# A two-layer GNN on one core: the tail after the edge loop in another order, and buffers of its own for the last edge pair

## The chip, the cores and the metric

The kernel runs on one core of a Trainium2 chip. The time is device microseconds of one execution. Of the kernel before there are three timed runs (median 1211.6 us) and one profiled execution of its own. PE is TensorE, DVE VectorE, ACT ScalarE, POOL GpSimd, SP SyncE.

## What is computed

There are 1250 nodes (padded to 1280, so 10 node tiles of 128) with 512 features, and 20000 edges. The first layer (a GIN block with batch norms) ends long before the change. The second layer is what matters here:

```python
h = jnp.maximum(_layernorm(x, axis=-1), 0.0)
edge_feat = jnp.concatenate([h[src], h[dst], edge_attr], axis=-1)
m = mish(mish(edge_feat @ W1 + b1) @ W2 + b2)       # 20000 x 512 messages
agg = jax.ops.segment_sum(m, dst, num_segments=h.shape[0])
u = mish(jnp.concatenate([h, agg], axis=-1) @ W3 + b3)
y = h + u @ W4 + b4
x = x + layernorm(y) * gamma + beta
```

## The kernel before

Every engine has one program, written out by hand in the order in which it runs; engines wait for each other by semaphores alone. Each f32 product is three fp32r products (high x low, low x high, high x high), so every operand is split first: a cast makes the high part, a subtraction the low part.

**The edge loop.** Edges go through in pairs of 128-edge tiles, 79 pairs (EDGE_PAIRS); the last, FINAL = 78, has one tile only. A pair s runs through z1 (PE), four ACT steps, h_full (DVE, L1677), z2 (PE), four ACT steps on the work buffer EB (exp2, sq2, log2, inv2: L1124 to L1136), `message` (DVE, L1700), `hi2` (cast, L1707), `lo2` (subtraction, L1711), and `segment1` (PE, L840), which adds the messages into a PSUM bank by a one-hot matrix (`hots1`, L1317). After every second pair `add_group` adds the bank into the node sums AGG with two DVE instructions (L1328). `load_range` (L1305) loads the rows of the next group into registers of DVE's sequencer. `more_of` is a branch for groups that span more tiles. In the last pair, exp2 waits for `message(FINAL - 1)`, since both use EB, and `hi2(FINAL)` waits until `segment1(FINAL - 1)` has read the message buffers.

**The aggregate is transposed.** Ten times: four PE transposes (`ag_t`, L696) into one of four PSUM banks, `ag_high` (ACT, L925), `ag_low` (DVE, L1298). `ag_t(nt)` can reuse a bank once `ag_low(nt - 4)` is done.

**The update.** 1280 nodes go in BLOCKS = 4 blocks of BW = 320 columns, each in two halves: half block n = 0 to 7. `u_product` (PE, 24 matmuls at L778) needs the transposed tiles of its block; then on DVE `u_start(n)` (L1791, adds the part from h), `u_bound(n)` (L1800, a cap at 20), four ACT steps (`u_mish`, L1176 to L1188), on DVE `u_end(n)` (L1806), on POOL `u_high(n)` (the cast, L573), on DVE `u_low(n)` (L1812).

**The rows.** `y_product(nt)` (PE, 12 matmuls at L884) makes the output rows of one node tile of 128. It needs `u_low` of the block in which its last node lies: tiles 0 and 1 need block 0, 2 to 4 block 1, 5 and 6 block 2, 7 to 9 block 3 (n = 6 and 7). `y_rows(nt)` on DVE: add to H (L1821), `bn_stats` (L1823), `bn_aggr` (L1824), and then, for nt < OUT_FIRST = 5, the mean negated (L1827, one column), and from 5 on (y - mean) * gamma over the whole row (L1829). `y_scale(nt)` on ACT makes rstd and scales the row (L1213 or L1217), for nt < 8 (OUT_LAST). `finish(nt)` on POOL multiplies by gamma (L578, nt < 5 only) and adds X (L580). The last two tiles end on DVE, `y_last` (L1835). SP sends each tile out in order (L454): tile 8 waits in SP's queue behind tile 7.

In DVE's program y_rows(0) and y_rows(1) stand ahead of u_end(4), y_rows(2) ahead of u_low(4), and so on to u_low(7), which stands behind y_rows(5). ACT has y_scale(0) ahead of u_mish(6) and y_scale(1) ahead of u_mish(7); POOL has finish(0) ahead of u_high(6) and finish(1) ahead of u_high(7).

## Time and profile before

| | us |
|---|---|
| three runs: median (lowest to highest) | 1211.6 (1210.19 to 1213.27) |
| the profiled execution | 1206.78 |
| its span, first to last instruction | 1204.7 |
| edge sums done, first transpose of the aggregate | 1126.56 |
| first `y_product` | 1161.65 |
| last DVE instruction ends | 1201.40 |

The span is 2.1 us shorter than the time of the same execution, which in its turn lies 4.8 us under the median of the three timed runs. All times inside are from the start of the span. Over the whole span PE is busy 91%, DVE 77%, ACT 75%, POOL 55%; but that is an average in which the edge loop (450 to 1120 us) holds most. The stretch that the change touches runs from 1117 us to the end.

### The profile page before, as it was taken

Reading aid. Unit: us, or ns where it says so; the run is one execution under the profiler, and the core shown is the slowest. Engines: PE = TensorE matmul, PEld = TensorE weight load, DVE = VectorE, ACT = ScalarE, POOL = GpSimd, SP = SyncE. Lnnn points to the kernel's source line nnn. Section 1 sums busy time; section 2 is a strip of 40 time slices with the busy share of each in tenths; the row PEclk is TensorE's granted clock in tenths of the full one; section 3 lists DMA queues with packets and bytes.
Section 4 is the critical chain, followed back from the end, with each engine's and each line's share of the span. In section 5 each row is a group of like instructions: output and inputs, shape, how many; then the busy total and the mean of one; then the engine's idle time right before and its main releaser. Section 6 shows DMA issues by size and latency. Waiting matters only on the chain.

```text
span 1204.7 us, 18542 instructions
## 1 busy us (share of the span) xinstructions
PE 1094.8 (91%) x5769; PEld 920.7 (76%) x5770; DVE 926.4 (77%) x1533; ACT 899.7 (75%) x1134; POOL 665.4 (55%) x534
## 2 busy tenths in 40 slices
PE   3664999889799979999999999999999999999795
PEld 0111888889777968888888888888888888888694
DVE  8997685463546148888889898998888888888688
ACT  7963462562350259999999999999999999998464
POOL 5877203000115357767688888888876767650116
PEclk9756999999889989999999999999999999999898
DMA  2005601030116346766666666666666666651002
GB/s 102 1 1 86 160 1 70 1 114 1 44 61 201 79 115 146 161 130 138 134 140 134 138 135 139 131 135 141 135 134 136 140 134 137 131 120 35 1 1 86
DMA packets 61086, 121.35 MB, mean 101 GB/s; under 512 B 7851, under 2 KB 18348, under 8 KB 60918
## 3 DMA queue, kind: packets, MB, share of 16 engines
q0 software_dynamic: 38048, 87.58, 35.8%
q1 hardware_dynamic: 22998, 33.28, 8.2%
q8 instruction: 20, 0.33, 0.1%
q14 instruction: 20, 0.16, 0.0%
HBM read 107.78 MB, written 7.80 MB: 96 GB/s over the span
## 4 chain that ended last, share of the span: by engine, by line
PE 81%; DVE 12%; ACT 3%; issue 2%; DVEq 1%; POOL 0%; ACTq 0%; POOLq 0%
PE banks L827 12%; PE banks L822 11%; PE banks L823 11%; PE banks L716 9%; PE banks L807 6%; PE banks L669 6%; PE banks L840 6%; PE banks L801 6%; PE banks L778 5%; PE banks L759 4%; DVE edge_counts L1484 3%; PE banks L820 3%; DVE key_onehot L1411 3%; PE banks L696 1%; PE banks L884 1%
## 5 line engine op out<-in xcount | busy, mean ns | idle before, releaser
L522 POOL DMA_INDIRECT gather_pq<-q_table,dst x157 | 299.0, 1904 | 58.1 <-issue 47.5
L514 POOL DMA_INDIRECT gather_pq<-p_table,src x157 | 175.2, 1116 | 157.4 <-PE banks L807 105.2
L822 PE MATMUL banks<-w_lo,h_hi 128*128 128x512 f32 x628 | 245.0, 390 | 0.0
L823 PE MATMUL banks<-w_hi,h_hi 128*128 128x512 f32 x628 | 244.7, 390 | 0.0
L827 PE MATMUL banks<-w_hi,h_lo 128*128 128x512 f32 x628 | 168.7, 390 | 0.0
L1677 DVE SCALAR_TENSOR_TENSOR h_full<-mish_work,banks 128x512 f32<-128x512 f32 (+1 forms) x158 | 101.0, 681 | 50.3 <-ACT mish_work L1118 47.7
L823 PEld LDWEIGHTS banks<-w_hi,h_hi 128*128 128x128 f32 x628 | 118.2, 188 | 25.6
L827 PEld LDWEIGHTS banks<-w_hi,h_lo 128*128 128x128 f32 x628 | 117.9, 188 | 24.5
L822 PEld LDWEIGHTS banks<-w_lo,h_hi 128*128 128x128 f32 x628 | 118.4, 189 | 22.2
L1106 ACT ACTIVATE mish_work<-banks 128x1024 f32<-128x1024 f32 (+1 forms) x79 | 80.7, 1021 | 31.6 <-PE banks L807 31.6
L1700 DVE SCALAR_TENSOR_TENSOR message<-mish_work,banks 128x1024 f32<-128x1024 f32 (+1 forms) x79 | 96.0, 1215 | 9.6 <-ACT mish_work L1136 1.7
L801 PE MATMUL banks<-ident,gather_pq 128*128 128x128 f32 x628 | 95.7, 275 | 6.9 <-DVE h_full L1677 6.8
L807 PE MATMUL banks<-edge_attr_parts,we_hi 128*128 128x256 f32 (+1 forms) x316 | 95.9, 325 | 2.4 <-DVE edge_attr_parts L1670 2.4
L1711 DVE TENSOR_TENSOR message_lo<-message,message_hi 128x1024 fp32r<-128x1024 f32 (+1 forms) x79 | 96.8, 1225 | 0.1
L1689 DVE TENSOR_TENSOR h_lo<-h_full,h_hi 128x1024 fp32r<-128x1024 f32 (+1 forms) x79 | 95.8, 1212 | 0.1
L801 PEld LDWEIGHTS banks<-ident,gather_pq 128*128 128x128 f32 x628 | 75.6, 141 | 18.0 <-issue 7.9
L479 POOL TENSOR_SCALAR src_onehot<-iota,src_parts 128x128 f16<-128x128 f32 x120 | 75.2, 640 | 25.2 <-PE banks L629 22.0
L629 PE MATMUL banks<-key_onehot,src_onehot 128*128 128x400 f16 x120 | 44.5, 501 | 47.5 <-DVE key_onehot L1411 39.0
L1114 ACT ACTIVATE mish_work<-mish_work 128x1024 f32<-128x1024 f32 (+1 forms) x79 | 83.5, 1057 | 2.5
L1110 ACT ACTIVATE mish_work<-mish_work 128x1024 f32<-128x1024 f32 (+1 forms) x79 | 83.4, 1056 | 2.5
L1132 ACT ACTIVATE mish_work<-mish_work 128x1024 f32<-128x1024 f32 (+1 forms) x79 | 83.4, 1056 | 2.5
L1136 ACT ACTIVATE mish_work<-mish_work 128x1024 f32<-128x1024 f32 (+1 forms) x79 | 83.1, 1052 | 0.1
(229 smaller groups left out, 2789.9 us busy)
## 6 DMA issues: line engine op xcount, KB each, us to landing
edge_attr<-in_edge_attr_t SPq DMA_DIRECT2D x79, 128.0 KB, 3.5
x_nodes<-h_hi POOLq DMA_DIRECT2D x10, 256.0 KB, 7.8
x_nodes<-h_lo POOLq DMA_DIRECT2D x10, 256.0 KB, 9.4
p_table<-p_stage SPq DMA_DIRECT2D x10, 256.0 KB, 2.0
q_table<-agg_nodes SPq DMA_DIRECT2D x10, 256.0 KB, 3.1
gather_pq<-p_table,src POOLq DMA_INDIRECT x157, 3.9
gather_pq<-q_table,dst POOLq DMA_INDIRECT x157, 4.9
x_nodes<-in_x SPq DMA_DIRECT2D x3, 768.0 KB, 6.2
```

Of the source, the lines that this page charges most:

```text
L514: nc.gpsimd.indirect_dma_start(GP[:, 2 * j + k, :], None, p_tab[:, :], bass.IndirectOffsetOnAxis(ap=SRC[:, 2 * s + k:2 * s + k + 1], axis= ...
L522: nc.gpsimd.indirect_dma_start(GP[:, 2 * j + k, :], None, q_tab[:, :], bass.IndirectOffsetOnAxis(ap=DST[:, 2 * s + k:2 * s + k + 1], axis= ...
L716: mm = pe.matmul(bank, weights[w][:, k, o * P:(o + 1) * P], acts[a](k)[:, nodes], start=(k == 0 and n == 0), stop=(k == kn - 1 and n == 2) ...
L801: pe.matmul(Z1v[:, c, k * P:(k + 1) * P], GP[:, 2 * slot + k, c * P:(c + 1) * P], IDENT[:, :], is_transpose=True, skip_group_check=True, s ...
L807: mm = pe.matmul(Z1v[:, c, 0:P * tiles(s)], w[:, c * P:(c + 1) * P], AT_R[:, j, 0:P * tiles(s)], skip_group_check=True, start=False, stop= ...
L822: pe.matmul(at, H_HI[:, j, c, e], W2_LO[:, c, :], start=False, stop=False)
L823: pe.matmul(at, H_HI[:, j, c, e], W2_HI[:, c, :], start=False, stop=False)
L827: mm = pe.matmul(at, H_LO[:, j, c, e], W2_HI[:, c, :], start=False, stop=(c == KD - 1))
L1677: nc.vector.scalar_tensor_tensor(HF[:, at[0], at[1]], EA[:, at[0], at[1]], -0.5, Z1v[:, at[0], at[1]], ALU.add, ALU.mult).then_inc(h_full[ ...
L1689: nc.vector.tensor_tensor(H_LO[:, j, :, 0:P * tiles(s)], HF[:, :, 0:P * tiles(s)], H_HI[:, j, :, 0:P * tiles(s)].bitcast(F32), ALU.subtrac ...
L1700: nc.vector.scalar_tensor_tensor(MSG[:, 0:tiles(s), :], EB[:, 0:tiles(s), :], -0.5, Z2[:, 2 * j:2 * j + tiles(s), :], ALU.add, ALU.mult).t ...
L1711: nc.vector.tensor_tensor(MSG_LO[:, 0:tiles(s), :], MSG[:, 0:tiles(s), :], MSG_HI[:, 0:tiles(s), :].bitcast(F32), ALU.subtract).then_inc(m ...
```

## The change

The last pair no longer shares buffers with the one before it: its ACT steps work in EA (the buffer of the first mish), its message goes into HF, its parts into slot 1 of H_HI and H_LO, and its one-hot matrix into a free piece of H_LO. exp2(FINAL) waits for h_full of the last pair in place of message(FINAL - 1). On DVE the adds of group FINAL - 1 stand behind all three message steps of FINAL, and load_range between the two add groups. PE runs six `ag_t` ahead of the first u_product in place of four. DVE's update becomes a period of four instructions per half block, with rows 0 and 1 between the last low parts and rows 2 to 9 behind them. ACT and POOL do all of the mish steps and casts ahead of the rows. The gamma product of rows 5 to 7 moves from DVE to POOL, and ACT gives those rows the bias that it gave rows 0 to 4.

```diff
         FINAL_SEG = BANKS[:, 0, :]
+        FINAL_WORK, FINAL_MSG = EA[:, 0:2, :], HF[:, 0:2, :]
+        FINAL_HI, FINAL_LO, FINAL_HOT = H_HI[:, 1, 0:2, :], H_LO[:, 1, 0:2, :], H_LO[:, 1, 2, 0:P]
...
+        def z2_out(s, j):
+
+            if isinstance(s, int) and s == FINAL:
+                return Z2[:, 2 * j, :].rearrange("p (c e) -> p c e", c=2)
+            return Z2[:, 2 * j:2 * j + 2, :]
...
             def finish(nt):
                 pool.wait_ge(norm_done, nt + 1)
-                if nt < OUT_FIRST:
-                    nc.gpsimd.tensor_tensor(H[:, nt, :], H[:, nt, :], ROWS[:, ROW_GAMMA, :], ALU.mult).then_inc(y_gamma, 1)
-                    pool.wait_ge(y_gamma, nt + 1)
+                nc.gpsimd.tensor_tensor(H[:, nt, :], H[:, nt, :], ROWS[:, ROW_GAMMA, :], ALU.mult).then_inc(y_gamma, 1)
+                pool.wait_ge(y_gamma, nt + 1)
                 nc.gpsimd.tensor_tensor(H[:, nt, :], H[:, nt, :], X[:, nt, :], ALU.add).then_inc(out_ready, 1)
 
 
             pool.wait_ge(tr_done, TR_AG + NT)
-            for n in range(6):
+            for n in range(UPAIRS * BLOCKS):
                 u_high(n)
-            finish(0)
-            u_high(6)
-            finish(1)
-            u_high(7)
-            for nt in range(2, OUT_LAST):
+            for nt in range(OUT_LAST):
                 finish(nt)
...
                 pe.wait_ge(msg_lo, s + 1)
-                bank = SEG[:, 0, :] if tiles(s) == 2 else FINAL_SEG
-                rows = MSG_ROWS[:2 * tiles(s)]
+                final = isinstance(s, int) and s == FINAL
+                bank, rows = (FINAL_SEG, FINAL_ROWS) if final else (SEG[:, 0, :], MSG_ROWS)
                 for n, row in enumerate(rows):
-                    mm = pe.matmul(bank, ONEHOT[:, j, n // 2, :], row, start=(j == 0 and n == 0), stop=(last and n == len(rows) - 1))
+                    hot = FINAL_HOT if final else ONEHOT[:, j, n // 2, :]
+                    mm = pe.matmul(bank, hot, row, start=(j == 0 and n == 0), stop=(last and n == len(rows) - 1))
                 mm.then_inc(seg_done, 1)
...
@@ -898,19 +904,15 @@
                 transpose_node(AGG, nt, ag_lo)
 
             pe.wait_ge(w3_lo, W3_PIECES)
-            for nt in range(4):
+            for nt in range(6):
                 ag_t(nt)
             u_product(0, 0)
-            ag_t(4)
-            ag_t(5)
-            u_product(0, 1)
             ag_t(6)
             ag_t(7)
-            u_product(1, 0)
+            u_product(0, 1)
             ag_t(8)
             ag_t(9)
-            u_product(1, 1)
-            for b in range(2, BLOCKS):
+            for b in range(1, BLOCKS):
                 for q in range(UPAIRS):
                     u_product(b, q)
...
+            def z2_work(s):
+                return FINAL_WORK if isinstance(s, int) and s == FINAL else EB[:, 0:2, :]
+
             def exp2(s, j):
                 act.wait_ge(z2_done, s + 1)
-                if after(s, 1):
+                if isinstance(s, int) and s == FINAL:
+                    for h in range(2):
+                        act.wait_ge(h_full[h], EDGE_PAIRS)
+                elif after(s, 1):
                     act.wait_ge(msg_full, s)
-                nc.scalar.activation(EB[:, 0:tiles(s), :], Z2[:, 2 * j:2 * j + tiles(s), :], ACT.Exp).then_inc(b_exp, 1)
+                nc.scalar.activation(z2_work(s), z2_out(s, j), ACT.Exp).then_inc(b_exp, 1)
...
@@ -1206,37 +1214,28 @@
                 if nt >= OUT_LAST:
                     return
                 act.wait_ge(rstd_ready, nt + 1)
-                if nt < OUT_FIRST:
-                    act.wait_ge(y_mean, nt + 1)
-                    nc.scalar.activation(NBIAS[:, nt:nt + 1], TMP[:, 0, nt:nt + 1], ACT.Identity, scale=RSTD[:, nt:nt + 1]).then_inc(y_shift, 1)
-                    act.wait_ge(y_shift, nt + 1)
-                    nc.scalar.activation(H[:, nt, :], H[:, nt, :], ACT.Identity, bias=NBIAS[:, nt:nt + 1],
-                                         scale=RSTD[:, nt:nt + 1]).then_inc(norm_done, 1)
-                else:
-                    act.wait_ge(gamma_done, nt - OUT_FIRST + 1)
-                    nc.scalar.activation(H[:, nt, :], H[:, nt, :], ACT.Identity, scale=RSTD[:, nt:nt + 1]).then_inc(norm_done, 1)
+                act.wait_ge(y_mean, nt + 1)
+                nc.scalar.activation(NBIAS[:, nt:nt + 1], TMP[:, 0, nt:nt + 1], ACT.Identity, scale=RSTD[:, nt:nt + 1]).then_inc(y_shift, 1)
+                act.wait_ge(y_shift, nt + 1)
+                nc.scalar.activation(H[:, nt, :], H[:, nt, :], ACT.Identity, bias=NBIAS[:, nt:nt + 1],
+                                     scale=RSTD[:, nt:nt + 1]).then_inc(norm_done, 1)
...
-            for nt in range(6):
+            for nt in range(7):
                 ag_high(nt)
             u_exponential(0)
-            ag_high(6)
+            ag_high(7)
             u_square(0)
-            ag_high(7)
+            ag_high(8)
             u_log(0)
-            ag_high(8)
+            ag_high(9)
             u_inverse(0)
-            ag_high(9)
-            for n in range(1, 6):
+            for n in range(1, UPAIRS * BLOCKS):
                 u_mish(n)
-            y_scale(0)
-            u_mish(6)
-            y_scale(1)
-            u_mish(7)
-            for nt in range(2, NT):
+            for nt in range(NT):
                 y_scale(nt)
...
-            for s in range(2 * (LAST - 1), FINAL + 2):
+            for s in range(2 * (LAST - 1), FINAL + 1):
                 edge_step(s, s % 2, s // 2)
 
+
+            hi2(FINAL - 2)
+            lo2(FINAL - 2)
+            hots1(FINAL - 1, 1)
+            dve.wait_ge(z2_done, FINAL)
+            make_hots([FINAL_HOT], REL_G, 2 * FINAL).then_inc(hot_ready, 1)
+            more_of(FINAL - 2, 0, EDGE_GROUPS - 2)
+            message(FINAL - 1, 1)
             hi2(FINAL - 1)
             lo2(FINAL - 1)
-            hots1(FINAL, 0)
-            message(FINAL, 0)
-            more_of(FINAL - 1, 0, EDGE_GROUPS - 2)
+            dve.wait_ge(b_r, EDGE_PAIRS)
+            dve.wait_ge(h_lo, EDGE_PAIRS)
+            nc.vector.scalar_tensor_tensor(FINAL_MSG, FINAL_WORK, -0.5, z2_out(FINAL, 0), ALU.add, ALU.mult).then_inc(msg_full, 1)
+            dve.wait_ge(msg_full, EDGE_PAIRS)
+            nc.vector.tensor_copy(FINAL_HI, FINAL_MSG).then_inc(msg_hi, 1)
+            dve.wait_ge(msg_hi, EDGE_PAIRS)
+            nc.vector.tensor_tensor(FINAL_LO, FINAL_MSG, FINAL_HI.bitcast(F32), ALU.subtract).then_inc(msg_lo, 1)
+            add_group(FINAL - 1, 0, EDGE_GROUPS - 2, SEG[:, 0, :])
+            more_of(FINAL - 1, 0, EDGE_GROUPS - 1)
             load_range(1, EDGE_GROUPS - 1)
-            hi2(FINAL)
-            lo2(FINAL)
-            add_group(FINAL - 1, 0, EDGE_GROUPS - 2, SEG[:, 0, :])
             add_group(FINAL, 1, EDGE_GROUPS - 1, FINAL_SEG)
             more_of(FINAL, 1, EDGE_GROUPS)
             wait_extras()
...
@@ -1823,7 +1831,7 @@
                 link(nc.vector.bn_stats(STATS[:, nt, 0:6], H[:, nt, :]))
                 nc.vector.bn_aggr(LN_MV[:, nt, :], STATS[:, nt, 0:6]).then_inc(var_ready, 1)
                 dve.wait_ge(var_ready, VAR_LN3 + nt + 1)
-                if nt < OUT_FIRST:
+                if nt < OUT_LAST:
                     nc.vector.tensor_scalar(TMP[:, 0, nt:nt + 1], LN_MV[:, nt, 0:1], -1.0, None, ALU.mult).then_inc(y_mean, 1)
                 else:
                     nc.vector.scalar_tensor_tensor(H[:, nt, :], H[:, nt, :], LN_MV[:, nt, 0:1], ROWS[:, ROW_GAMMA, :],
...
             def y_last(nt):
                 dve.wait_ge(rstd_ready, nt + 1)
-                dve.wait_ge(gamma_done, nt - OUT_FIRST + 1)
+                dve.wait_ge(gamma_done, nt - OUT_LAST + 1)
                 nc.vector.scalar_tensor_tensor(H[:, nt, :], H[:, nt, :], RSTD[:, nt:nt + 1], X[:, nt, :], ALU.mult, ALU.add).then_inc(out_last, 1)
 
-            for nt in range(6):
+            for nt in range(7):
                 ag_low(nt)
             u_start(0)
             u_bound(0)
-            ag_low(6)
+            ag_low(7)
             u_start(1)
             u_bound(1)
-            for nt in range(7, NT):
-                ag_low(nt)
-            u_start(2)
-            u_start(3)
-            for n in range(4):
-                u_end(n)
-                u_bound(n + 2)
-                u_start(n + 4)
-                u_low(n)
+            ag_low(8)
+            ag_low(9)
+            for n in range(2, UPAIRS * BLOCKS):
+                u_end(n - 2)
+                u_start(n)
+                u_bound(n)
+                u_low(n - 2)
+            u_end(6)
             y_rows(0)
+            u_low(6)
+            u_end(7)
             y_rows(1)
-            u_end(4)
-            u_bound(6)
-            y_rows(2)
-            u_low(4)
-            u_end(5)
-            u_bound(7)
-            y_rows(3)
-            u_low(5)
-            u_end(6)
-            y_rows(4)
-            u_low(6)
-            y_rows(5)
-            u_end(7)
             u_low(7)
-            for nt in range(6, NT):
+            for nt in range(2, NT):
                 y_rows(nt)
                 if nt >= OUT_LAST:
                     y_last(nt)
```

The edge loop's own body (the Fori) is the same instruction by instruction on every engine, and SP's program is the same throughout. Line numbers below are those of each kernel.

DVE at the last pair. Before, the message of the last pair (128x512), its load of tile_range, then its parts and the adds:

```order
L1707 CAST message_hi<-message 128x1024
L1711 TENSOR_TENSOR message_lo<-message,message_hi 128x1024
L1317 TENSOR_SCALAR onehot<-iota,dst_in_group 128x128
L1700 SCALAR_TENSOR_TENSOR message<-mish_work,banks 128x512
...
L1305 TENSOR_LOAD tile_range
L1707 CAST message_hi<-message 128x512
L1711 TENSOR_TENSOR message_lo<-message,message_hi 128x512
L1325 ISA
L1328 SCALAR_TENSOR_TENSOR agg_nodes<-banks,from_low,agg_nodes 128x512
...
L1328 SCALAR_TENSOR_TENSOR agg_nodes<-banks,from_low,agg_nodes 128x512
```

After, the same place (L1778 to L1782 are the last pair's three steps, L1327 the adds):

```order
L1699 SCALAR_TENSOR_TENSOR message<-mish_work,banks 128x1024
L1705 CAST message_hi<-message 128x1024
L1709 TENSOR_TENSOR message_lo<-message,message_hi 128x1024
L1778 SCALAR_TENSOR_TENSOR h_full<-mish_work,banks 128x512
L1780 CAST h_hi<-h_full 128x512
L1782 TENSOR_TENSOR h_lo<-h_full,h_hi 128x512
L1324 ISA
L1327 SCALAR_TENSOR_TENSOR agg_nodes<-banks,from_low,agg_nodes 128x512
...
L1304 TENSOR_LOAD tile_range
L1324 ISA
L1327 SCALAR_TENSOR_TENSOR agg_nodes<-banks,from_low,agg_nodes 128x512
```

The first adds have moved behind the last pair's parts, and the register load to between the two groups of adds.

DVE at the end of the update. Before, from the low part of half block 3 on:

```order
L1812 TENSOR_TENSOR u_t_lo<-u_t,u_t_hi 128x2x320
L1821 SCALAR_TENSOR_TENSOR h_nodes<-banks,h_nodes 128x512
L1823 BN_STATS stats<-h_nodes 128x6
L1824 BN_AGGR ln_mean_var<-stats 128x2
L1827 TENSOR_SCALAR tmp<-ln_mean_var 128x1
L1821 SCALAR_TENSOR_TENSOR h_nodes<-banks,h_nodes 128x512
L1823 BN_STATS stats<-h_nodes 128x6
L1824 BN_AGGR ln_mean_var<-stats 128x2
L1827 TENSOR_SCALAR tmp<-ln_mean_var 128x1
L1806 SCALAR_TENSOR_TENSOR u_t<-mish_work_88,u_t 128x2x320
L1800 TENSOR_SCALAR mish_work_88<-u_t 128x640
L1821 SCALAR_TENSOR_TENSOR h_nodes<-banks,h_nodes 128x512
```

After, from the cap of half block 7 on (L1820 is the low part, L1814 u_end, L1829 to L1835 y_rows):

```order
L1808 TENSOR_SCALAR mish_work_89<-u_t 128x640
L1820 TENSOR_TENSOR u_t_lo<-u_t,u_t_hi 128x2x320
L1814 SCALAR_TENSOR_TENSOR u_t<-mish_work_88,u_t 128x2x320
L1829 SCALAR_TENSOR_TENSOR h_nodes<-banks,h_nodes 128x512
L1831 BN_STATS stats<-h_nodes 128x6
L1832 BN_AGGR ln_mean_var<-stats 128x2
L1835 TENSOR_SCALAR tmp<-ln_mean_var 128x1
L1820 TENSOR_TENSOR u_t_lo<-u_t,u_t_hi 128x2x320
L1814 SCALAR_TENSOR_TENSOR u_t<-mish_work_89,u_t 128x2x320
L1829 SCALAR_TENSOR_TENSOR h_nodes<-banks,h_nodes 128x512
L1831 BN_STATS stats<-h_nodes 128x6
```

Before, two whole y_rows stand ahead of the u_end of half block 4; after, the first y_rows stands behind the u_end of half block 6.

POOL behind the last edge. Before (L573 is u_high, L578 and L580 are finish):

```order
L573 CAST u_t_hi<-u_t 128x2x320 x6
L578 TENSOR_TENSOR h_nodes<-h_nodes,rows 128x512
L580 TENSOR_TENSOR h_nodes<-h_nodes,x_nodes 128x512
L573 CAST u_t_hi<-u_t 128x2x320
L578 TENSOR_TENSOR h_nodes<-h_nodes,rows 128x512
L580 TENSOR_TENSOR h_nodes<-h_nodes,x_nodes 128x512
L573 CAST u_t_hi<-u_t 128x2x320
```

After (L580 is u_high, L584 and L586 are finish):

```order
L580 CAST u_t_hi<-u_t 128x2x320 x8
L584 TENSOR_TENSOR h_nodes<-h_nodes,rows 128x512
L586 TENSOR_TENSOR h_nodes<-h_nodes,x_nodes 128x512
L584 TENSOR_TENSOR h_nodes<-h_nodes,rows 128x512
L586 TENSOR_TENSOR h_nodes<-h_nodes,x_nodes 128x512
L584 TENSOR_TENSOR h_nodes<-h_nodes,rows 128x512
```

All eight casts now stand ahead of the first finish, and each of the eight finish has two instructions (before, five had two and three had one).

## Rows read from the trace of the kernel before

**Rows 1.** Chain of work that ended last: start us, us, engine, tile, line.
```profile
1117.28 1.23 DVE message L1700
...
1121.49 0.75 DVEq L1305
...
1134.57 0.87 PE banks L696 x8
...
1161.81 5.48 PE banks L884 x24
```

**Rows 2.** Timeline, DVE at the last edges: start us, us, what, [idle before <-releaser].
```profile
1118.42 0.48 DVE L1317 TENSOR_SCALAR onehot<-iota,dst_in_group 128x128 fp32r<-128x128 f32 x2
...
1121.22 0.69 DVE L1700 SCALAR_TENSOR_TENSOR message<-mish_work,banks 128x512 f32<-128x512 f32 x1 [0.26 <-ACT mish_work L1136]
...
1122.36 0.43 DVE L1707 CAST message_hi<-message 128x512 fp32r<-128x512 f32 x1 [0.45 <-PE banks L840]
...
1125.05 0.75 DVE L1328 SCALAR_TENSOR_TENSOR agg_nodes<-banks,from_low,agg_nodes 128x512 f32 x1 [0.22 <-DVE agg_nodes L1328]
```

**Rows 3.** Timeline, ACT at the last edges.
```profile
1115.98 1.06 ACT L1136 ACTIVATE mish_work<-mish_work 128x1024 f32<-128x1024 f32 x1
1118.60 0.60 ACT L1124 ACTIVATE mish_work<-banks 128x512 f32<-128x512 f32 x1 [1.56 <-DVE message L1700]
```

**Rows 4.** Timeline, PE from the transposes to the last row.
```profile
1126.56 3.43 PE L696 MATMUL banks<-ident,agg_nodes 128*128 128x128 f32 x16 [1.78 <-issue]
1130.77 0.42 PE L778 MATMUL banks<-agg_t_lo,w_hi 128*128 128x320 f32 x1 [0.78 <-DVE agg_t_lo L1298]
...
1161.65 0.39 PE L884 MATMUL banks<-w_hi,u_t_lo 128*128 128x512 f32 x1
...
1178.57 0.50 PE L884 MATMUL banks<-w_hi,u_t_lo 128*128 128x512 f32 x1 [1.78 <-DVE u_t_lo L1812]
...
1187.79 0.80 PE L884 MATMUL banks<-w_hi,u_t_lo 128*128 128x512 f32 x1 [3.46 <-DVE u_t_lo L1812]
...
1196.02 0.39 PE L884 MATMUL banks<-w_hi,u_t_hi 128*128 128x512 f32 x1
```

**Rows 5.** Timeline, DVE from the first row to its last instruction.
```profile
1164.59 0.69 DVE L1821 SCALAR_TENSOR_TENSOR h_nodes<-banks,h_nodes 128x512 f32<-128x512 f32 x1 [1.19 <-PE banks L884]
...
1185.86 1.87 DVE L1812 TENSOR_TENSOR u_t_lo<-u_t,u_t_hi 128x640 fp32r<-128x640 f32 x1 [0.81 <-POOL u_t_hi L573]
...
1193.73 0.69 DVE L1821 SCALAR_TENSOR_TENSOR h_nodes<-banks,h_nodes 128x512 f32<-128x512 f32 x1
...
1198.13 0.68 DVE L1821 SCALAR_TENSOR_TENSOR h_nodes<-banks,h_nodes 128x512 f32<-128x512 f32 x1
...
1200.65 0.75 DVE L1835 SCALAR_TENSOR_TENSOR h_nodes<-h_nodes,rstd,x_nodes 128x512 f32<-128x512 f32 x1
```

**Rows 6.** Timeline, ACT: the scaling that ends y_scale(0).
```profile
1167.16 0.82 ACT L1213 ACTIVATE h_nodes<-h_nodes,ln_bias,rstd 128x512 f32<-128x512 f32 x1
```

**Rows 7.** Groups by line, 1161.6 to 1205: busy us, mean ns of one, idle before.
```profile
L1806 DVE SCALAR_TENSOR_TENSOR u_t<-mish_work,u_t 128x640 f32<-128x640 f32 x4 | 3.3, 816 | 0.0
...
L1180 ACT ACTIVATE mish_work<-mish_work 128x640 f32<-128x640 f32 x3 | 2.2, 739 | 0.1
```

**Rows 8.** One line's instructions: duration in ns (min/median/max), first and last start.
```profile
L580 POOL TENSOR_TENSOR h_nodes<-h_nodes,x_nodes x8: 1267/1666/1764, 1176.6 to 1197.6; 128x512 f32<-128x512 f32 x8
L578 POOL TENSOR_TENSOR h_nodes<-h_nodes,rows x5: 1263/1290/1537, 1175.0 to 1191.8; 128x512 f32<-128x512 f32 x5
L1800 DVE TENSOR_SCALAR mish_work<-u_t x8: 493/1025/1028, 1137.7 to 1174.3; 128x640 f32<-128x640 f32 x8
```

**Rows 9.** Windows: us, busy of PE, PEld, DVE, ACT, POOL (instructions), PEclk, DMA, GB/s.
```profile
1131.00:1140.00 9.00, 9.00 (x67) 8.99 (x67) 2.86 (x5) 2.40 (x5) 0.00 (x0) 1.00 0.00 0
1189.00:1192.00 3.00, 3.00 (x11) 2.34 (x10) 2.79 (x5) 1.23 (x3) 2.92 (x3) 0.66 0.23 87
```

**Rows 10.** SP's ten issues of output tiles: duration in ns, first and last start.
```profile
L454 SPq DMA_DIRECT2D out_x<-h_nodes x10: 332/332/431, 1177.9 to 1201.4; - x10
```

22 lines of the change are left out of this document (11 added, 11 removed).

## The prediction, made before the changed kernel was timed

> **What bounds the kernel now.** I read the page's chain of waits first: it lies on PE through the edge loop, and the loop's body is unchanged, so only the stretch behind it counts. I read that stretch as the chain in order of time, then each engine's timeline, and asked at each idle piece what ended it. There are four places.
>
> (a) The last edge pair. exp2 of the last pair could start only when DVE's message of pair 77 was done, with ACT idle 1.56 us before it [rows 3]; the DVE message that follows waits 0.26 us for ACT, the cast behind it starts only when the register load of 0.75 us (1121.49 to 1122.24) is over [rows 1, 2], and the last adds end at 1125.05 + two instructions of 0.7 = 1126.46; the first transpose starts at 1126.56 [rows 4].
> (b) PE idles 0.78 us before the first u_product [rows 4].
> (c) The two stalls inside the rows: PE waits 1.78 and 3.46 us for a low part of u on DVE [rows 4]. The low part stands late in DVE's program, behind y_rows that have no hurry, and the ACT and POOL steps that it needs stand behind y_scale and finish. After the second stall PE runs at its lower level: the granted clock is 0.66 in 1189 to 1192, where it was 1.00 in 1131 to 1140 [rows 9].
> (d) The end. PE's last matmul starts at 1196.02 and ends at 1196.41 [rows 4], but y_rows(9) begins only at 1198.13, since DVE is still at tile 8, and its last instruction ends at 1201.40 [rows 5]. The span ends 3.3 us later (1204.7), with the last transfer landing.
>
> **The sum, step by step**, against the profiled execution (span 1204.7, time 1206.78).
>
> *Last edge pair.* DVE is free for the next step at 1117.28 [rows 1]. In the new order it then has: three one-hots, 0.24 each by the pair of 0.48 [rows 2], 0.65 with the third; message of 77, 1.23 [rows 1]; its cast and its subtraction, 0.7 and 1.25 (the 128x1024 subtraction as long as the message of the same shape); the last pair's message 0.69, cast 0.43 [rows 2], subtraction 0.7; four adds, two pairs of 1.41. That is 8.5 us, and DVE never waits for ACT in it: exp2 can start when ACT is free at 1117.04 [rows 3], and its four steps, 2.6 us (1118.60 to the message at 1121.22 [rows 2, 3]), are done at 1119.7, while DVE asks for them at 1121.1. The register load now lies between the two pairs of adds. It runs on the sequencer while the last add of the first pair executes, so it costs between 0 and 0.75; I take 0.4, as the gap that it left before the cast is 0.45 [rows 2]. The adds end at 1117.28 + 8.9 = 1126.2 in place of 1126.46: **0.3 us** (0 to 0.7). So DVE's own work is next behind the wait that goes, and most of ACT's 1.56 us is not won.
>
> *Transposes 4 and 5.* They move into the idle 0.78 us and out from behind u_product(0,0), where eight of them took 0.87 [rows 1]. In the new place they follow the first 16, which took 3.43, that is 0.21 each at the lower clock level [rows 4]: eight cost 0.87 to 1.7. Gain 0.78 + 0.87 - (0.87 to 1.7) = -0.06 to 0.78; I take **0.35**. The first y_product starts at 1161.65 - 0.3 - 0.35 = **1161.0**. In between PE runs 8 products without a wait before, and should after: DVE's period per half block is u_end 0.82 [rows 7], u_start and the low part as long (the same 128x640), and the cap 0.49, or 1.03 where POOL's cast runs beside it [rows 8], that is 3.0 to 3.5 us, against 3.5 us of a u_product (from 1130.77 to 1161.65 PE has eight of them and three times 0.87 of transposes [rows 1, 4]).
>
> *PE through the rows.* 24 matmuls take 5.48 us [rows 1], 0.228 each; 120 start within 27.1 us and the last ends at 1161.0 + 27.1 + 0.4 = **1188.5** if nothing stalls, against 1196.41: 7.9 us, of which 0.65 is from above. Does anything stall? y_product(7) starts 19 us behind the first. Its low part is behind: y_product(0) done and y_rows(0) begun, 2.94 us after the first matmul (1164.59 - 1161.65 [rows 4, 5]); two y_rows of 1.8; u_low(6), u_end(7), u_low(7) of 0.8, one of them up to 1.87 when it meets POOL [rows 5]. Sum 8.9 to 10 us: 9 us early. ACT's mish of half block 7 (four steps of 0.74 [rows 7]) and POOL's cast fit into the same time. This is the step on which the forecast rests.
>
> *DVE at the end.* y_rows(8) begins one y_product (2.7) before the end of PE's work, at 1185.9. Tile 8 took 4.40 us (1193.73 to 1198.13) beside POOL's additions, tile 9 3.27 us (1198.13 to 1201.40) nearly without them, since POOL's last starts at 1197.6 and lasts 1.7 [rows 5, 8]. If POOL is still at work for tile 8 and just done for tile 9, y_rows(9) begins at 1190.3, and the last DVE instruction ends at 1193.6 to 1194.7; I take **1193.8**.
>
> *POOL at the end.* It is the engine that gets more: three gamma products of 1.29 [rows 8] and all eight finish behind the last cast. Tile 2's scaling is done about 13.3 us after the first y_product (the 9.9 us above for u_low(7), 1.7 for y_rows(2) up to its mean, 1.7 for ACT, 1166.27 to 1167.98 [rows 6]), so finish(2) starts at 1174.3 and six finish follow back to back. Two instructions with the medians 1.29 and 1.67 [rows 8] are 3.0 us: POOL ends at 1192.3. SP then sends tiles 7 and 8, 0.33 us each [rows 10], and has tile 9's place free before 1193.8. So POOL is 0.8 us off the path.
>
> Here a rule bears on the sum. What the rows show: POOL's X addition took 1.27 at least and 1.67 in the median, DVE's low part 1.87 where PE's stall ended [rows 5, 8]. The Trainium skill (SBUF — State Buffer, Who interferes with whom) says that a VectorE instruction with two SBUF inputs and a GpSimd instruction that reads SBUF exclude each other for the whole instruction, while one with a single SBUF input does not meet GpSimd. By that rule rows 0 to 7 of the new order, whose VectorE steps read PSUM and one SBUF tensor, would leave a finish at 2 x 1.35 = 2.7 us and POOL would end near 1190.5; by the medians above it ends at 1192.3. The sum goes by the medians.
>
> *The end.* 1193.8 + 3.3 = 1197.1. Three transfers may come close together; each 256 KB, so I allow 0 to 0.5 and take 0. **1204.7 - 1197.1 = 7.6 us**: 0.3 and 0.35 ahead of the rows, about 7.0 from the two stalls and the slow matmuls behind the second. The profiled execution would come out at 1199.2. The median of the timed runs stands 4.8 us above the profiled one; I take the same difference off it: 1211.6 - 7.6 = **1204.0 us**.
>
> **The rivals.**
>
> *POOL becomes the end.* For: it has 16 instructions after the casts, and those beside DVE lasted up to 1.76 us [rows 8]. Two of 1.76 are 3.6 us with the wait between: six finish end at 1174.3 + 21.7 = 1196.0, SP's two issues ahead of tile 9 make 1196.7, and 3.3 more 1200.0. Gain 4.7: 1206.9. Against: only the X addition was long in the median. It decides from a finish of 3.13 us (1193.8 - 0.7 - 1174.3, by six).
>
> *A stall stays.* The change would not do what it says if y_product(7) still had to wait, for instance because ACT or DVE is late by a whole queue. The second stall with its slow matmuls cost about 5 us: gain 2.6, 1209.0, which nobody could tell from no change. Against: 9 us of slack, worked out above.
>
> *PE at the lower clock level through the rows, slower than before.* PE comes to the transposes from idle in both kernels; if the level did not rise for the rows, each of the 120 matmuls would cost 0.2 us more (the 0.228 of [rows 1] doubled, nearly), 24 us in all: 1228. It decides from 38 slow matmuls (7.6 by 0.2) for no gain at all, and from 56 for slower by over 0.3%. Against: in this trace the level is 1.00 wherever PE has been at work without a break [rows 9] and low only behind idle pieces, of which the change has fewer.
>
> *The last pair gains nothing* is no case of its own: it is worth 0.3.
>
> **How the numbers follow.** Forecast 0.74; POOL the end 0.15; a stall stays 0.08; low clock 0.03. Range: in the forecast's own case the gain is 6.0 (no gain at the last pair, -0.06 for the transposes, tile 9 fully beside POOL, 0.9) to 9.8 (0.4 and 0.43 more there, tile 8 at 3.27 and not 4.40, 0.2 at tile 9), 1201.8 to 1205.6. It reaches to POOL's case, 1206.9, and the three timed runs spread 1.5 us to either side of their median; so 1201.0 to 1207.5. Some 0.3% (3.6 us) is what a measurement of this kernel can tell from no change. Faster by more than that: the first two cases less a little for the spread, 0.88; within it 0.09; slower 0.03.
>
> **What would show it.** Right: in the profile after, L884's counterpart has no idle piece that a low part of u ended, the granted clock is 1.00 from the first u_product to the last y_product, ACT's exp2 of the last pair starts near 1117.1, and the first y_product near 1161.0. POOL's last addition ends before 1193, DVE's last instruction near 1193.8. Wrong: tile 7's issue on SP behind DVE's end (POOL is the end); PE idle again before tile 7 (a stall stays); DVE idle for ACT between two caps; or a first y_product at 1162 or later, which would say that the transposes at the lower level cost more than the idle piece that they fill.

## The result: 1199.4 us, below the predicted range

The changed kernel took 1199.43 us in the median of four executions (1199.41 to 1199.84), the kernel before 1211.01: a ratio of 0.9902, 95% interval 0.9885 to 0.9919. The forecast was 1204.0, the range began at 1201.0. In the profiled execution the span is 1197.6 us (time 1199.44), and the page's chain of waits, taken in order of time, now ends so (start us, us, engine, tile, line, count):

```profile
1122.71 3.01 PE banks L844 x6
1125.72 2.49 issue
1128.21 4.41 PE banks L698 x24
1132.62 3.58 PE banks L780 x24
1137.07 3.51 PE banks L780 x24
1141.46 21.11 PE banks L780 x144
1162.57 24.52 PE banks L890 x108
1188.79 1.27 DVE h_nodes L1837
1190.17 1.55 DVE h_nodes L1843
```

Where [rows 4] had stalls of 1.78 and 3.46 us, the update's last 144 matmuls and those of the rows follow each other without a break. DVE is ready for each row, and what it waits for is PE. Its timeline (start us, us, operation, idle before and what ended it) answers to [rows 5]:

```profile
1165.36 0.69 DVE L1829 SCALAR_TENSOR_TENSOR h_nodes<-banks,h_nodes 128x512 f32<-128x512 f32 x1
...
1184.40 0.69 DVE L1829 SCALAR_TENSOR_TENSOR h_nodes<-banks,h_nodes 128x512 f32<-128x512 f32 x1 [0.90 <-PE banks L890]
...
1187.12 0.69 DVE L1829 SCALAR_TENSOR_TENSOR h_nodes<-banks,h_nodes 128x512 f32<-128x512 f32 x1 [0.89 <-PE banks L890]
...
1190.17 1.55 DVE L1843 SCALAR_TENSOR_TENSOR h_nodes<-h_nodes,rstd,x_nodes 128x512 f32<-128x512 f32 x1
1191.64 0.68 DVE L1829 SCALAR_TENSOR_TENSOR h_nodes<-banks,h_nodes 128x512 f32<-128x512 f32 x1
...
1194.16 0.75 DVE L1843 SCALAR_TENSOR_TENSOR h_nodes<-h_nodes,rstd,x_nodes 128x512 f32<-128x512 f32 x1
```

A row comes every 2.72 us. DVE ends at 1194.91, the span 2.7 us behind it. POOL's gamma and X additions, against [rows 8]:

```profile
1170.77 1.76 POOL L586 TENSOR_TENSOR h_nodes<-h_nodes,x_nodes 128x512 f32<-128x512 f32 x1
1172.48 1.30 POOL L584 TENSOR_TENSOR h_nodes<-h_nodes,rows 128x512 f32<-128x512 f32 x1
1173.86 1.29 POOL L586 TENSOR_TENSOR h_nodes<-h_nodes,x_nodes 128x512 f32<-128x512 f32 x1
1175.11 1.28 POOL L584 TENSOR_TENSOR h_nodes<-h_nodes,rows 128x512 f32<-128x512 f32 x1
...
1189.58 1.59 POOL L586 TENSOR_TENSOR h_nodes<-h_nodes,x_nodes 128x512 f32<-128x512 f32 x1
```

One row costs POOL 2.63 us, and it ends at 1191.17.

**One execution is not like the other.** The gain between the two profiled executions is 7.3 us, between the medians 11.6. To find the rest I cut each profiled execution at the same instructions into four stretches: *ahead* (up to DVE's split of message 76, the third from the end: the subtraction `lo2`), *adds* (to the start of the last pair of additions onto the aggregated nodes), *transposes* (to the start of the update's first addition), *rows* (to the end of the span). *Adds* to *rows* together are called the tail below. The labels are those of the experiments below.

| kernel, execution | time | ahead | adds | transposes | rows |
|---|---|---|---|---|---|
| before, first | 1206.78 | 1115.95 | 9.10 | 11.83 | 67.82 |
| before, e1 | 1208.65 | 1117.43 | 9.74 | 11.81 | 67.82 |
| before, e8 | 1212.40 | 1121.55 | 9.10 | 11.81 | 67.84 |
| before, e11 | 1207.87 | 1117.00 | 9.11 | 11.83 | 67.86 |
| before, e12 | 1209.87 | 1118.40 | 9.74 | 11.81 | 67.85 |
| before, e13 | 1211.48 | 1117.92 | 9.74 | 14.17 | 67.87 |
| before, e14 | 1210.05 | 1118.82 | 9.74 | 11.82 | 67.82 |
| before, e15 | 1210.26 | 1117.51 | 9.10 | 14.00 | 67.89 |
| changed, first | 1199.44 | 1117.73 | 8.97 | 11.21 | 59.69 |
| changed, e5 | 1199.83 | 1117.91 | 8.97 | 11.42 | 59.70 |
| changed, e16 | 1199.42 | 1118.40 | 8.27 | 11.22 | 59.71 |

*Rows* is the same to 0.1 us in each execution: 67.85 before, 59.70 after, 8.15 us of gain. *Adds* and *transposes* have two or more values each. *Ahead*, where no line was changed, has the mean 1118.07 before and 1118.01 after, but a spread of 5.6 us, and the first profile, against which the prediction's sum was made, is the lowest of the eight.

### The profile page after: what moved, and what is told of

It is laid out like the page before. It is cut to its first block, busy times and chain, and to the rows that moved or that the text cites. A ratio compares the mean times of both kernels' runs of the same rounds, so it can differ in the third digit from the quotient of the medians.

```text
span 1197.6 us, 18547 instructions
## 1 busy us (share of the span) xinstructions
PE 1096.4 (92%) x5769; PEld 921.8 (77%) x5770; DVE 919.9 (77%) x1533; ACT 901.0 (75%) x1137; POOL 665.7 (56%) x537
## 4 chain that ended last, share of the span: by engine, by line
PE 83%; DVE 10%; ACT 3%; issue 2%; DVEq 1%; POOL 0%; ACTq 0%; POOLq 0%
PE banks L829 12%; PE banks L824 12%; PE banks L825 12%; PE banks L718 9%; PE banks L809 6%; PE banks L844 6%; PE banks L671 6%; PE banks L803 6%; PE banks L780 5%; PE banks L761 4%; DVE edge_counts L1483 3%; PE banks L822 3%; DVE key_onehot L1410 3%; PE banks L890 2%; PE banks L698 1%
## 5 line engine op out<-in xcount | busy, mean ns | idle before, releaser
L1699 DVE SCALAR_TENSOR_TENSOR message<-mish_work,banks 128x1024 f32<-128x1024 f32 x78 | 95.3, 1221 | 9.2 <-ACT mish_work L1144 1.4
L1709 DVE TENSOR_TENSOR message_lo<-message,message_hi 128x1024 fp32r<-128x1024 f32 x78 | 96.1, 1232 | 0.1
```

The costliest lines, as they stand in the source:

```text
L1699: nc.vector.scalar_tensor_tensor(MSG[:, :, :], EB[:, :, :], -0.5, z2_out(s, j), ALU.add, ALU.mult).then_inc(msg_full, 1)
L1709: nc.vector.tensor_tensor(MSG_LO[:, :, :], MSG[:, :, :], MSG_HI[:, :, :].bitcast(F32), ALU.subtract).then_inc(msg_lo, 1)
```

## The experiments

**e1, the kernel before once more** (no edit).

> The kernel before, once more, unchanged, to see how its executions spread. Theory one (the body is luck): what GpSimd's long cast and subtraction of W3 do to VectorE's additions near 370 to 395 us differs by some us from execution to execution, so timed executions stand anywhere from 1206 to 1213 us and the stretch from 360 to 395 us in this profile is longer or shorter than in the first by as much as the whole execution is. Theory two (the tail is luck): the rows stage of the old tail, with its stalls of 1.78 and 3.46 us on TensorE, costs more in some executions, so the stretch up to 1116 us repeats within 1 us, and a longer execution shows its excess behind 1160 us. Theory three (the first profile was the odd one): every execution now stands at 1210 to 1213 us and none near 1206.8.

Median 1210.42 us of eleven (1208.65 to 1211.68). Over all executions of the kernel before in this study (79) the median is 1210.4, the mean 1210.5, and the range 1206.2 to 1214.5. The choice of chip is not the source: series of eleven or more on different chips have medians of 1210.2 to 1210.7, and eleven on one chip lie between 1206.2 and 1214.2. The first theory explains a part. It is about the Q stage, in which PE multiplies the ten node tiles by a part of W1 and DVE takes each product out of PSUM (into agg_nodes) and makes two additions of its own. DVE in the first profile, and in e1:

```profile
381.16 2.53 DVE L1665 TENSOR_TENSOR h_nodes<-h_nodes,rows 128x512 f32<-128x512 f32 x1
383.61 0.68 DVE L1663 TENSOR_TENSOR agg_nodes<-banks,rows 128x512 f32<-128x512 f32 x1
384.21 4.49 DVE L1664 TENSOR_TENSOR x_nodes<-x_nodes,rows 128x512 f32<-128x512 f32 x1
```

```profile
379.22 2.51 DVE L1664 TENSOR_TENSOR x_nodes<-x_nodes,rows 128x512 f32<-128x512 f32 x1
381.66 5.03 DVE L1665 TENSOR_TENSOR h_nodes<-h_nodes,rows 128x512 f32<-128x512 f32 x1
386.62 0.68 DVE L1663 TENSOR_TENSOR agg_nodes<-banks,rows 128x512 f32<-128x512 f32 x1
```

Two additions of 0.68 us take 2.5 and 4.5 to 5 while POOL casts (1.9 us) and splits (4.9 us) the first half of W3, the update's weights. In the first profile they happened to fall so that DVE took a product out of PSUM between them (383.61); in e1 it came to that only at 386.62. The nodes' last product leaves PSUM 1.7 us later. Of the eight profiles of the table's upper half only e11 has the order of the first: there PE waits 1.97 us, in the first 1.98, in the other six 3.43, and these two have the shortest *ahead*. The second theory falls as it was put, since *rows* is the same (67.82 in both); but 0.64 us of e1's excess do lie in the tail, in *adds* (9.74 and not 9.10). The third theory falls, with 1208.65 in this run.

**e2, the last pair alone.** The buffers FINAL_WORK to FINAL_HOT and the new order of DVE's last edge steps, with the update and the rows as before:

```
+        FINAL_WORK, FINAL_MSG = EA[:, 0:2, :], HF[:, 0:2, :]
...
-            for s in range(2 * (LAST - 1), FINAL + 2):
+            for s in range(2 * (LAST - 1), FINAL + 1):
```

> Only the part for the last edge pair (its buffers, its order on VectorE, ScalarE and TensorE); the rows and the update stay as before. By the prediction 0.3 us less than the kernel before; by the trace of the changed kernel, in which the additions of the last pair ended only 0.13 us nearer to the end of the pair ahead, 0.1 us less. In either case under what a timed comparison tells. If instead the excess of the timed executions of the kernel before over its profiled one came from the old rows stage, this kernel spreads from 1206 to 1213 us as the kernel before does.

1208.69 us of eleven (1207.21 to 1211.09), ratio 0.9980 (0.9971 to 0.9989): a gain of 1.3 to 3.5 us that can be told, contrary to both expectations. *Adds* took 8.96, *transposes* 11.82, *rows* 67.90. The spread stayed (3.9 us), which decides nothing here, since this kernel has the old rows; that they are not its source the *rows* column shows, with 67.82 to 67.90 in all nine profiles. The gain in time is more than the 0.8 us that the stretches give for this part (worked out below), and its one profile does not show where the rest lies.

**e3, the update and rows alone** (the remaining pieces of the change).

> Only the new order of the update and the rows (transposes, VectorE's periods, gamma and X on GpSimd); the last edge pair as before. Against its own profile this should take 7.3 us of the 7.6 predicted, or 8.8 of the 8.9 us that the trace of the changed kernel shows from the last pair but one to the end. If the spread of the kernel before comes from its rows stage, the executions of this one agree within 0.5 us, as the four of the changed kernel did, at about 1199.5 us, and the timed gain is 11 to 12 us. If the spread comes from the stage at 370 to 395 us, this kernel spreads over 3 to 6 us like the kernel before.

1200.73 us of five (1199.41 to 1202.42). Its stretches are 9.10, 11.21 and 59.70: the old *adds*, the new rest. So the two parts add up piece by piece. The spread is 3.0 us, so the first expectation, executions within 0.5 us, falls.

**e4, W3 in pieces, before.**

```
-            nc.gpsimd.tensor_copy(W3A_HI, WA[:, 0:KD, :]).then_inc(w3a_hi, 1)
+            for k in range(KD):
+                nc.gpsimd.tensor_copy(W3A_HI[:, k, :], WA[:, k, :]).then_inc(w3a_hi, 1)
```

and the subtraction likewise.

> The kernel before with GpSimd's cast and subtraction of the first half of W3 (128x2048, 1.9 and 4.9 us of one instruction) each split into four of 128x512. If one long instruction of GpSimd holds off VectorE's additions of two SBUF tiles near 381 us (5.04 us for one of them in the changed kernel, 4.49 in the kernel before, and 0.8 to 1 us when nothing holds them off), the additions now wait for at most a piece of 1.3 us, the TensorE stall of 3.4 us on the aggregated nodes near 380 us shrinks, and the kernel is 1 to 3 us faster. If the spread of timed executions comes from that lock, it also goes to under 1 us. If neither, time and spread are those of the kernel before.

1211.45 us, ratio 1.0005 (0.9996 to 1.0015): nothing won. The timelines of POOL and of DVE say why:

```profile
380.33 2.29 POOL L532 CAST w_lo<-weights_a 128x512 fp32r<-128x512 f32 x4
382.59 4.97 POOL L535 TENSOR_TENSOR w_hi<-weights_a,w_lo 128x512 fp32r<-128x512 f32 x4
```

```profile
380.28 7.83 DVE L1666 TENSOR_TENSOR x_nodes<-x_nodes,rows 128x512 f32<-128x512 f32 x1
```

One addition was held until the last of eight pieces had ended. Cutting POOL's instruction into pieces did not let DVE in between them. This profile also has the long *transposes* that e13 and e15 show below (14.14 us).

**e5, the changed kernel once more** (no edit).

> The changed kernel once more, unchanged. Theory of the tail's clock (TensorE's granted clock behind its stalls stays low for a stretch whose length differs between executions, and the old rows stage has two more such stalls): the spread of this kernel is smaller than the 5 us of the kernel before, but not nothing, since the stalls behind the last edge pairs are still there: 1199.4 to about 1202.5 us, as the kernel with the new tail alone (1199.4 to 1202.4). Theory of the body (GpSimd's long cast and subtraction of W3 against VectorE's additions at 380 us): the body is the same in both kernels, so this one spreads over as many us as the kernel before. If the four executions seen so far (1199.4 to 1199.8) tell the truth, it does not spread at all.

1200.17 us of six (1197.74 to 1200.76); with the first four and e16, eleven executions have the median 1199.4, the mean 1199.7. It does spread, over 3.0 us.

**e6, TensorE kept busy, changed kernel.** Unread matmuls ahead of the last two segments and of the transposes:

```
+            def keep_busy(n):
+                for _ in range(n):
+                    pe.matmul(BANKS[:, 1, :], W3B_HI[:, 0, 0:P], W3B_HI[:, 0, :], start=True, stop=True)
...
+                if s == EDGE_PAIRS + 2:
+                    pe.wait_ge(w3_lo, W3_PIECES)
+                    keep_busy(8)
+                if s == EDGE_PAIRS + 3:
+                    keep_busy(7)
...
+            keep_busy(6)
```

> The changed kernel with matmuls whose result nobody reads, put where TensorE would wait for the last messages and for the aggregated nodes: 8 ahead of the last segment but one, 7 ahead of the last, 6 ahead of the transposes (128x512 each, 0.23 us at the full clock, 0.43 at the low one). Theory of the tail's clock: the granted clock, 0.50 from 1122 to 1130 us and 0.92 from 1130 to 1140 us in the profile of the changed kernel, stays at 1.00; 24 transposes take 2.2 to 3 us where they took 4.41, the kernel is 1 to 2.5 us faster and its executions agree better. If the clock has nothing to do with how busy TensorE is, or the added matmuls come in the way of the segments, it is the same or up to 1 us slower.

1198.69 us of six (1197.85 to 1201.13). PE's windows (us, length, busy and instructions, granted clock, DMA share, GB/s) in the changed kernel, then in e6:

```profile
1122.00:1130.00 8.00, 4.80 (x15) 0.50 0.00 0
1130.00:1140.00 10.00, 10.00 (x71) 0.92 0.00 0
```

```profile
1122.00:1130.00 8.00, 6.70 (x37) 1.00 0.00 0
1130.00:1140.00 10.00, 10.00 (x73) 1.00 0.01 2
```

The clock stays at the full level and *adds* plus *transposes* fall from 20.2 to 18.9 us (from 19.5 against e16, which had the shorter *adds*). That TensorE's idle time there brings the low clock, and the low clock costs time, is shown; the gain in the median, 0.7 us, is under what six executions tell. The spread stayed at 3.3 us, so it does not come from here in this kernel.

**e7, W3's cast on ScalarE, the split paced, changed kernel.**

```
-            pool.wait_ge(w3a_in, 16)
-            nc.gpsimd.tensor_copy(W3A_HI, WA[:, 0:KD, :]).then_inc(w3a_hi, 1)
             pool.wait_ge(w3a_hi, 1)
-            nc.gpsimd.tensor_tensor(W3A_LO, WA[:, 0:KD, :], W3A_HI.bitcast(F32), ALU.subtract).then_inc(w3a_lo, 1)
+            for k in range(KD):
+                pool.wait_ge(q_moved, 4 + k)
+                nc.gpsimd.tensor_tensor(W3A_LO[:, k, :], WA[:, k, :], W3A_HI[:, k, :].bitcast(F32), ALU.subtract).then_inc(w3a_lo, 1)
...
+            act.wait_ge(w3a_in, 16)
+            nc.scalar.copy(W3A_HI, WA[:, 0:KD, :]).then_inc(w3a_hi, 1)
```

> The changed kernel with the cast of the first half of W3 on ScalarE (which has nothing to do from 365 to 399 us) and GpSimd's subtraction in four pieces of 128x512, one for each of four tiles of the Q stage, each started when VectorE has taken a tile's result out of PSUM. In one profile of the cut into pieces that follow each other at once, VectorE's addition was held for 7.83 us, the whole of GpSimd's row of eight; so it is the gap between GpSimd's instructions that lets VectorE in, not their length. With a tile every 2.72 us and VectorE busy for 2.0 us of it, a piece of 1.25 us per tile should be taken in almost wholly: TensorE's two waits for agg_nodes (3.4 us in sum) go, the first edge pair starts about 3 us earlier, and the kernel is 2.5 to 3.5 us faster. If the time of the Q stage does not reach the end of the kernel (the edge loop waits for gathers instead), it is the same.

1193.90 us of five (1192.38 to 1195.22), ratio to the kernel before 0.9862 (0.9843 to 0.9882): 5.5 us under the changed kernel, more than was expected. From 380 to 398 us PE was busy for 14.57 of 18 us; now, with DVE's held additions of the paced pieces:

```profile
380.00:398.00 18.00, 18.00 (x93) 1.00 0.34 114
```

```profile
379.36 3.16 DVE L1665 TENSOR_TENSOR x_nodes<-x_nodes,rows 128x512 f32<-128x512 f32 x1
...
384.25 1.78 DVE L1666 TENSOR_TENSOR h_nodes<-h_nodes,rows 128x512 f32<-128x512 f32 x1
```

The 3.4 us of idle TensorE that the expectation counted are gone, and with them what it had left out, the low clock behind them: 0.91 on the mean over these 18 us in the changed kernel, which by that share is 1.6 us (an estimate). The last product leaves PSUM at 392.69 us, in e5 at 397.86. Which of the two edits, the cast on ACT or the pacing, gives how much was not tried.

**e8, e11 to e15: the kernel before, six more profiles** (no edit).

> The kernel before, a third profile. By the theory of the tail's clock its length follows from two stretches: the low clock behind the last edge pairs (to 1130 us in the first profile, further in others) and behind the stall of 3.46 us in the rows; by the theory of the body from the Q stage (VectorE's held additions). The profile shows which of the two carries what this execution is above 1206.8 us.

> The kernel before, a fourth profile. The three so far split their length so: to the split of the last message but two 1115.95, 1117.43 and 1121.55 us, from there to the end 88.75, 89.37 and 88.75 us. If the excess of the timed executions (1210.5 us in the middle of 54) over the first profiled one (1206.8) lies ahead of the tail, this execution too has a tail of 88.7 to 89.4 us and the rest ahead; if it lies in the tail, some have tails of 90 to 91 us, as the kernel with W3 in pieces did (91.1).

> The kernel before, a fifth profile, for the same question as the fourth, with the same two answers: a tail of 88.7 to 89.4 us with the rest of the excess ahead of it, or a tail of 90 to 91 us.

> The kernel before, a sixth profile. Five so far: 1115.95, 1117.43, 1121.55, 1117.00 and 1118.40 us to the split of the last message but two, and tails of 88.75, 89.37, 88.75, 88.80 and 89.40 us. The tail of the changed kernel took 79.87 and 80.09 us, so the tail explains 9.0 of the 10.9 us between the medians (1210.5 and 1199.6). If the other 1.9 us are old tails with a longer stretch at the low clock, which the five happened to miss, one or two of the next three have a tail over 90 us; if they lie ahead of the tail, the tails stay at 88.7 to 89.4 and the executions above 1210 us have more than 1119.5 us ahead of it.

> The kernel before, a seventh profile, for the same question and with the same two answers as the sixth.

> The kernel before, an eighth profile, for the same question and with the same two answers as the sixth.

The table has them. e8's excess lies ahead of the tail, by neither of the places named: against e1 it is 2.8 us late by 218 us (the batch norm) and 1.3 more by 452 us (the first edge pairs), each time behind a stall, with PE at the low clock (0.77 in 207 to 222 us, where e1 has 0.89). e13 and e15 show the long *transposes*. PE in e11, then in e13:

```profile
1127.62 3.34 PE L696 MATMUL banks<-ident,agg_nodes 128*128 128x128 f32 x16 [1.78 <-issue]
1131.83 0.42 PE L778 MATMUL banks<-agg_t_lo,w_hi 128*128 128x320 f32 x1 [0.87 <-DVE agg_t_lo L1298]
1132.08 0.31 PE L778 MATMUL banks<-agg_t_hi,w_lo 128*128 128x320 f32 x1
```

```profile
1129.17 3.65 PE L696 MATMUL banks<-ident,agg_nodes 128*128 128x128 f32 x16 [1.78 <-issue]
1133.38 0.64 PE L778 MATMUL banks<-agg_t_lo,w_hi 128*128 128x320 f32 x1 [0.56 <-DVE agg_t_lo L1298]
1133.81 0.47 PE L778 MATMUL banks<-agg_t_hi,w_lo 128*128 128x320 f32 x1
```

In e13 the first product of the update starts at the low level too, and 17 of its 24 matmuls take 0.47 and not 0.31. The granted clock from 1130 to 1140 us is 0.57, in e11 0.97:

```profile
1130.00:1140.00 10.00, 9.44 (x44) 0.57 0.00 0
```

This costs 2.2 to 2.3 us, in two of eight (and in e4). The Trainium skill (TensorE: Matmul & The Clock Gate, Part 1: The HAM clock gate) says that the span over which TensorE's activity is judged runs freely, so that the number of slow matmuls behind a start differs from run to run of one kernel. The traces agree on the number (none of these 24 matmuls at 0.47 us in e11, 17 in e13); what it depends on no row shows.

**e9, TensorE kept busy, before** (the edit of e6 with 8, 5 and 6 matmuls).

> The kernel before with unread matmuls ahead of the last segment but one (8), the last (5) and the transposes (6), and nothing else. The theory that the old tail loses more in other executions than in the profiled one because TensorE runs at the low clock behind these stalls (to 1130 us in one profile, over the whole of 1130 to 1140 us in another): the low clock there goes, the kernel is 1 to 3 us faster than the kernel before in the median, about as much as the last pair's buffers alone gave (1208.7 against 1210.5 us), and its tail from the split of the last message but two to the end is 87.5 us in every execution. The theory that the excess is all ahead of the tail (batch norm, Q stage, first edge pairs): its median falls by no more than the 0.5 us that the two shorter tails of the kernel before would lose, and its spread stays.

1208.62 us of twelve, ratio 0.9987 (0.9978 to 0.9995): 0.6 to 2.7 us of gain. Clock 1.00 from 1122 to 1140 us, *transposes* 10.95, *rows* 67.79. The tail was 87.85, 0.35 above what was expected. The spread, 4.1 us, stayed, which fits with *ahead* as its larger part.

**e10, both additions, changed kernel** (the edits of e6 and e7).

> The changed kernel with both additions: W3's cast on ScalarE with GpSimd's subtraction paced by the tiles of the Q stage, and the unread matmuls ahead of the last segments and the transposes. The two stand at different places (380 us and 1120 us) and nothing of the one is waited for by the other, so the gains should add: 5.7 us and 0.9 us under the changed kernel's 1199.6, 1193.0 us, with a tail of 78.6 us. If the clock behind the stall depends on when in an execution it comes, the second may be anything from 0 to 2.5 us.

1192.99 us of four (1191.75 to 1193.53), ratio to the kernel before 0.9857 (0.9843 to 0.9872), tail 78.5. The fastest version of the study, 6.4 us under the changed kernel; that the e6 part adds anything to e7 cannot be told from the times.

**e16, the changed kernel, a third profile** (no edit).

> The changed kernel, a third profile. By either answer its tail is 79.8 to 80.2 us if its one stall ahead of the transposes costs the same each time (0.92 mean clock from 1130 to 1140 us in the first). If what lies ahead of the tail has the same distribution in both kernels, since no line of it was changed, this may be anything from 1115.9 to 1121.5 us; if the changed kernel is really luckier there, it is again 1117.6 to 1117.9 us.

*Adds* is 8.27 and not 8.97, so the tail is 79.2, below the expected band; 1118.40 ahead of it is above the band of the luckier kernel.

**e17, gamma on GpSimd, old order.**

```
-        OUT_FIRST = NT // 2
+        OUT_FIRST = OUT_LAST
```

> The kernel before with one line changed: gamma of rows 5 to 7 goes to GpSimd as that of rows 0 to 4 (the row from which VectorE takes gamma over is 8 and no longer 5); VectorE's order is the old one. From the first addition of the update to the end, eight profiles of the old tail took 67.82 to 67.89 us and four of the new one 59.69 to 59.71. If the gain of 8.1 us comes from the order on VectorE (the split of the last half block no longer late for TensorE), this one takes no more than 1 to 2 us off the 67.8: the waits of 1.78 and 3.46 us stay, and VectorE ends behind the last product. If it comes from taking the three gammas (0.75, 1.33 and 1.17 us) off VectorE, 3 us or more go.

*Rows* took 70.78: 2.9 us slower than before, where both expectations were faster. POOL now works without a pause to 1205.35, and DVE's two-input instructions wait for it:

```profile
1197.92 1.76 DVE L1829 SCALAR_TENSOR_TENSOR h_nodes<-h_nodes,ln_mean_var,rows 128x512 f32<-128x512 f32 x1
1199.79 1.55 DVE L1835 SCALAR_TENSOR_TENSOR h_nodes<-h_nodes,rstd,x_nodes 128x512 f32<-128x512 f32 x1
...
1202.92 1.31 DVE L1829 SCALAR_TENSOR_TENSOR h_nodes<-h_nodes,ln_mean_var,rows 128x512 f32<-128x512 f32 x1
1204.34 1.56 DVE L1835 SCALAR_TENSOR_TENSOR h_nodes<-h_nodes,rstd,x_nodes 128x512 f32<-128x512 f32 x1
```

```profile
1203.76 1.59 POOL L580 TENSOR_TENSOR h_nodes<-h_nodes,x_nodes 128x512 f32<-128x512 f32 x1
```

DVE's gamma at 1197.92 began beside POOL's X addition and ended 0.55 us behind it, although POOL's next instruction follows without a gap:

```profile
1197.85 1.28 POOL L580 TENSOR_TENSOR h_nodes<-h_nodes,x_nodes 128x512 f32<-128x512 f32 x1
1199.09 1.71 POOL L578 TENSOR_TENSOR h_nodes<-h_nodes,rows 128x512 f32<-128x512 f32 x1
```

Tile 9 starts as late behind the update's first addition as before (61.35 against 61.25 us); DVE ends 1.5 us later than then, and the span another 1.5 us behind that (4.8 us, not 3.3). TensorE's waits stay, at 1.78 and 2.86 us.

**e18, gamma of rows 5 to 7 on VectorE, new order** (in y_rows, y_scale, finish and y_last of the changed kernel, the tests of nt against OUT_FIRST = NT // 2 as in the kernel before).

> The changed kernel with gamma of rows 5 to 7 left on VectorE, as it was, and everything else new. If the order does the work, TensorE still never waits in the rows, and the loss is what three gammas of 0.75 to 1.3 us put on VectorE where a row needs 1.76 us of 2.72: with them 3.0 us, so row 8 starts about 0.5 to 1 us later and the stretch from the update's first addition to the end takes 60 to 61 us. If taking the gammas away is what counts, it takes 63 us or more. By its rule for GpSimd beside VectorE the gammas on VectorE also hold back GpSimd's additions, and the other way round: then each is a few tenths longer than 0.75 us.

*Rows* 59.42, 0.3 us less than the changed kernel, where a loss was expected. TensorE never waits. DVE's gammas take 1.15 to 1.54 us beside POOL, where it had waited 0.9 us for each row, so tile 8 begins 0.7 us later behind the update's first addition than in the changed kernel. It gets this back at its last step, which takes 0.75 and not 1.55, since POOL, with three gammas fewer, has ended:

```profile
1184.04 1.37 DVE L1843 SCALAR_TENSOR_TENSOR h_nodes<-h_nodes,ln_mean_var,rows 128x512 f32<-128x512 f32 x1
...
1190.98 0.75 DVE L1849 SCALAR_TENSOR_TENSOR h_nodes<-h_nodes,rstd,x_nodes 128x512 f32<-128x512 f32 x1
```

So the new order carries all 8.15 us, and moving the gammas costs in either order. How much of it is DVE's order and how much that of ACT and POOL, which put all mish steps and casts ahead of the rows, no run separates: e17 has all the old orders and e18 all the new ones.

## Why the prediction was wrong, step by step

The mechanism was right: TensorE's two stalls go and DVE's last tiles become the end. The time was outside the range because the base and three terms of the sum (the last pair, the transposes, the end) were off the same way; the range missed by 1.6 us, and none of the four is that large. By means, 1204.0 against 1199.7:

- **The base, 1.1 us.** 1211.6 was a median of three, of a kernel whose executions lie from 1206.2 to 1214.5; over 79 the mean is 1210.5. "I take the same difference off it" carried the gain of one profiled execution to that number. The difference of 4.8 us was no property of the kernel: the first profile was the luckiest of eight ahead of the tail.
- **The last pair: 0.3 predicted, 0.8 measured.** The first profiles seem to show less than 0.3 (*adds* 9.10 and 8.97), but they are at different clock levels. Like against like it is 9.10 to 8.27 with the segment of pair 77 on PE at the full clock and 9.74 to 8.97 at the low one. The sum of DVE's steps was too large by 0.4. It took 0.4 for the register load between the two pairs of adds; the gap there is 0.22 us, and the old order has the same 0.22 [rows 2] without a load in it, so the load cost nothing that can be seen, and a gap was left out. Besides, back-to-back instructions start up to 0.1 us before the one ahead ends. Another 0.2 is DVE's start, 1.15 and not 1.33 us behind the split of message 76. "DVE never waits" held for ACT, but at the low clock it waits 0.62 us for the segment on PE, a wait that the text did not have. By the times the part may be worth more: e2's series gave 1.3 us at least, and by the means of all executions it is 1.7 from the kernel before to e2 and 1.2 from e3 to the changed kernel, with 0.8 and 1.2 to either side.
- **Transposes 4 and 5: 0.35 predicted, 0.9 measured.** *Transposes* went from 11.82 to 11.22, and from there to the first row another 0.26 (27.71 to 27.45). 24 transposes took 4.41 us where 16 had taken 3.43, so the eight cost 0.98, near the cheap end (0.87) of the bounds; 1.3 had been taken. Another 0.15 lies between the first y_product and its row on DVE (2.94 us before, 2.79 after). In two of eight executions of the old tail the first products ran at the low clock as well, 2.3 us more, which adds 0.6 to the mean gain; none of the six profiles with the new tail and no added matmuls (e3, e7 and e18 with the three of the table) has it, which six cannot prove.
- **PE without a stall, the step on which the forecast rested: right.** 27.1 us for the rows' matmuls was foreseen, and the chain shows 108 in 24.52 us with nothing before them; the granted clock is 1.00 from 1132.6 to 1189.8 us. The first y_product starts at 1162.57, later than the 1162 that was named as a sign of being wrong; but *ahead* was 1.78 us longer than in the first profile, and less that it is 1160.8, where 1161.0 was foreseen.
- **DVE at the end: 29.9 us foreseen from the first row to DVE's end, 29.55 measured. The rest behind DVE: 3.3 foreseen, 2.7 measured.** Together 0.9 us. Tile 8 took 4.52 us, near the 4.40 taken, and began 0.2 us earlier; tile 9 took 3.27 us, and not the 3.5 of the sum. What stands behind DVE goes with how early tile 7 is ready for SP: POOL ended 3.7 us ahead of DVE and 2.7 us followed, in the first profile 2.1 and 3.3, in e17 0.55 and 4.8. That the last transfers share something fits with this, but was not followed up.
- **POOL: 3.0 us per row foreseen by medians, 2.63 measured.** That is near the 2.7 of the rule of the Trainium skill (SBUF — State Buffer, Who interferes with whom) that the text set beside it. The trace agrees: only the first addition (beside a low part) and the last (beside tile 8) exceeded 1.3 us. The prediction told the rule too widely, though: an instruction of DVE with one SBUF input was longer beside POOL too, the cap with 1.03 us beside the cast and 0.49 without [rows 8]. POOL was off the path in both, so the time did not hang on it. e17 shows the rival "POOL becomes the end" coming true, with the old order.

The terms: base 1.1; last pair and transposes 1.0 like against like, and 0.4 more for the mix of clock levels; the end 0.9. That leaves 0.9 us of the 4.3. The stretches give 10.0 us of gain (0.7, 1.1 and 8.15, with 0.06 ahead), the means of all executions 10.8, with 0.6 to either side by their scatter (1.4 us in 79, 0.8 us in 11), and eight profiles leave *ahead* uncertain by more than 1 us. The remainder stays open; chance is enough for it, and the times of e2 and e3 point at the last pair. The range's own fault: it was made of the terms' bounds, and for the kernel's spread it had 1.5 us from three executions.

## What to carry to other kernels

Cut several profiled executions at the same instructions before a gain of 0.5% is worked out: here one stretch repeated to 0.1 us and the others by 0.6 to 5.6, and two profiles compared at different clock levels hid most of a term. What a stall costs is its idle time and the slow matmuls behind it, and the second part varies between executions. Where VectorE has slack for each tile, the order of its instructions and of those that feed it is worth more than moving instructions off it: here 8.15 us against a loss. And a long unbroken row of GpSimd instructions can be paid by VectorE's next instruction with two SBUF inputs: moving the cast to ScalarE and pacing the rest by VectorE's own progress won 5.5 us (e7).

## What the runs showed of the hardware

- A two-input VectorE instruction can be held for a whole row of GpSimd instructions and not for one of them alone (7.83 us for eight in e4). A small one is held as well: in the batch norm of the changed kernel, an instruction of one element per partition takes 8.87 us beside GpSimd's split of another weight. DVE and POOL:

```profile
201.82 8.87 DVE L1291 TENSOR_TENSOR bn_shift<-cols,tmp 128x1 f32<-128x1 f32 x1
```

```profile
201.65 9.02 POOL L505 TENSOR_TENSOR w_lo<-weights_b,w_hi 128x4096 fp32r<-128x4096 f32 x1
```

  ScalarE waits 8.2 us behind it and TensorE 3.9. Every profile of this study has such an instruction there, of 8.8 to 9.0 us, and no run tried to free it.
- Instructions that GpSimd starts one by one on semaphores, as in the rows, hold VectorE's gamma for 1.15 to 1.76 us and not for the whole row of them, in e17 even where the trace shows no gap between two of GpSimd's. What makes the difference to e4 was not tried by itself.
- What TensorE's low clock takes behind the stalls ahead of the transposes differed by 2.2 us between executions of one kernel (*transposes* 11.81 in e8 and 14.00 in e15), with the three stalls of PE ahead of them the same (2.40, 1.54 and 1.78 us in both).
